# Moving the second normalisation's statistics to ScalarE and staging the front two slots earlier in a fused attention and expert kernel

## What is computed

```python
x = x + attention(layernorm(x))
#   Q, K, V = projections, 16 heads of 8; scores = Q K^T, causal mask, no softmax
#   out = (scores * causal) V, then the output projection with its bias
x = x + experts(layernorm(x))
#   probs = softmax(x @ Wg) over 8 experts, the two largest kept
#   each token's result is the sum over its two experts of
#   prob * (relu(x @ W1[e] + b1[e]) @ W2[e] + b2[e])
```

## Time and profile before

| | |
|---|---|
| runs shown | 308.76, 564.43 and 1236.85 us, median 564.43 us |
| profiled execution, span (the only time it has) | 350.7 us |
| TensorE busy | 234.8 us, 67% |
| VectorE busy | 207.1 us, 59% |
| ScalarE busy | 140.9 us, 40% |
| GpSimd busy | 198.4 us, 57% |
| TensorE's granted clock, mean | 0.854 of full speed |

### The profile page before, as it was taken

One profiled execution on the slowest core, in us unless ns is written; L12 is line 12 of the kernel. 1 busy time (PEld: TensorE's weight loads), 2 busy tenths in 40 slices (PEclk: granted clock), 3 DMA queues, 4 the chain that ended last, 5 costly groups with the idle time before them and its releaser, 6 DMA issues.

```text
span 350.7 us, 6314 instructions
## 1 busy us (share of the span) xinstructions
PE 234.8 (67%) x1320; PEld 174.7 (50%) x1320; DVE 207.1 (59%) x745; ACT 140.9 (40%) x509; POOL 198.4 (57%) x184
## 2 busy tenths in 40 slices
PE   0799999999998999574300685977677686665000
PEld 0345666666565655363100675976567685554000
DVE  6888887989898989654541043434333443343074
ACT  2434566566565554342200363444343544342000
POOL 3465644588888888744673045554564455646300
PEclk9999999999999999855555599689898989999555
DMA  7910000000010101101121332223223232201199
GB/s 218 304 57 0 3 0 3 3 31 30 31 33 30 33 30 33 53 31 38 39 84 60 72 99 70 71 71 76 68 72 84 62 78 65 81 28 39 50 358 317
DMA packets 32399, 25.48 MB, mean 73 GB/s; under 512 B 4305, under 2 KB 30169, under 8 KB 32364
## 3 DMA queue, kind: packets, MB, share of 16 engines
q1 hardware_dynamic: 23808, 14.52, 15.2%
q0 software_dynamic: 4320, 8.47, 7.6%
q10 hardware_dynamic: 4236, 2.10, 2.0%
HBM read 13.92 MB, written 11.61 MB: 73 GB/s over the span
## 4 chain that ended last, share of the span: by engine, by line
issue 52%; PE 27%; DMA 5%; SPq 4%; ACT 3%; DVE 2%; ACTq 1%; another core or an unknown queue 1%; POOL 1%; DVEq 1%; POOLq 0%
PE ps L824 14%; PE ps L832 9%; PE ps L817 4%; DMA back<-returned 3%; ACT hT L458 3%; SPq L271 2%; SPq L289 2%; DMA bias_bc<-b_o 1%; DMA returned<-y_sb,xt 1%; POOL outer L324 1%; DMA xt<-dispatched 1%; DMA dispatched<-padding 1%; PE ps L709 0%; DVEq L243 0%
## 5 line engine op out<-in xcount | busy, mean ns | idle before, releaser
L349 POOL DMA_INDIRECT returned<-y_sb,xt x71 | 70.2, 988 | 70.9 <-DVE y_sb L685 51.3
L324 POOL TENSOR_TENSOR outer<-qkv 128x1024 f32<-128x1024 f32 x32 | 62.6, 1957 | 32.4 <-ACT qkv L404 32.0
L340 POOL DMA_INDIRECT dispatched<-rows,slot x64 | 62.5, 976 | 25.1 <-issue 15.4
L680 DVE TENSOR_TENSOR yb<-ps,b_bc 128x128 f32<-128x128 f32 x71 | 20.7, 291 | 77.2 <-PE ps L832 32.8
L824 PE MATMUL ps<-xT,w_of 128*128 128x128 f32 x284 | 51.1, 308 | 18.7 <-ACT hT L458 12.5
L739 PE MATMUL ps<-outer,causal 128*128 128x512 f32 x128 | 62.4, 610 | 0.0
L832 PE MATMUL ps<-w_sb,hT 128*128 x284 | 50.0, 304 | 16.3 <-ACT hT L458 10.3
L452 ACT ACTIVATE xT<-ps 128x128 f32<-128x128 f32 x71 | 19.8, 279 | 91.7 <-PE ps L817 72.1
L824 PEld LDWEIGHTS ps<-xT,w_of 128*128 128x128 f32 x284 | 42.8, 216 | 23.0 <-ACT xT L452 16.4
L832 PEld LDWEIGHTS ps<-w_sb,hT 128*128 128x128 f32 x284 | 42.3, 214 | 20.1 <-issue 19.9
L458 ACT ACTIVATE hT<-ps,b_col 128x128 f32<-128x128 f32 x142 | 44.4, 370 | 4.7 <-remote 3.0
(11 more groups left out here) (115 smaller groups left out, 355.5 us busy)
## 6 DMA issues: line engine op xcount, KB each, us to landing
xt<-dispatched SPq DMA_DIRECT2D x71, 65.0 KB
back<-returned SPq DMA_DIRECT2D x8, 512.0 KB, 7.6
x_sb<-x SPq DMA_DIRECT2D x8, 256.0 KB, 5.2
out<-x_sb ACTq DMA_DIRECT2D x8, 256.0 KB, 6.6
returned<-y_sb,xt POOLq DMA_INDIRECT x71, 2.3
w_sb<-w SPq DMA_DIRECT2D x1, 1024.0 KB, 5.6
w_sb<-w SPq DMA_DIRECT2D x2, 512.0 KB, 7.2
dispatched<-rows,slot POOLq DMA_INDIRECT x64
```

The lines of the kernel that those rows point to most:

```text
L324: pool.tensor_tensor(outer[:, g % OUTER_RING, :].rearrange("p (h b a) -> p h b a", h=HEADS, b=DH), k, v, ALU.mult).then_inc(outer_done, 1)
L340: pool.indirect_dma_start(out=dispatched[:, :], out_offset=bass.IndirectOffsetOnAxis(ap=slot[:, g * K + k:g * K + k + 1], axis=0), in_=row ...
L349: pool.indirect_dma_start(out=returned[:, :], out_offset=bass.IndirectOffsetOnAxis(ap=xt[:, n % G, D:D + 1].bitcast(I32), axis=0), in_=y_s ...
```

## The change

The statistics of the second normalisation leave VectorE. ScalarE now makes the negated mean with an `Identity` that scales by -1/128 and accumulates over the row, and the sum of squared deviations with a `Square` whose bias is that mean and which accumulates too. The Ln takes 1/128 as its scale. The shift becomes an `Identity` on ScalarE, and so do the four instructions that write the probabilities; these have lag 13 on ScalarE. ScalarE's and TensorE's front stages have lags smaller by two, `outer` gets a ring of 4 and `qkv` one of 12, and the waits that guard shared banks are moved by the same two tiles. GpSimd's list is as before.

```diff
-    OUTER_RING = 3
-    QKV_RING = 2 * T
+    OUTER_RING = 4
+    QKV_RING = 3 * T
...
+            def mean2_out(g):
+                wait(act, x2_done, g + 1)
+                act.activation(unread[:, 0, :], tile(g), ACT.Identity, scale=-1.0 / D,
+                               accum_out=mean2[:, g:g + 1]).then_inc(mean2_done, 1)
+
+            def spread2_out(g):
+                wait(act, mean2_done, g + 1)
+                act.activation(unread[:, 1, :], tile(g), ACT.Square, bias=mean2[:, g:g + 1],
+                               accum_out=spread2[:, g:g + 1]).then_inc(spread2_done, 1)
...
+            def shift2_out(g):
+                wait(act, rstd2_done, g + 1)
+                act.activation(norm2[:, g, 1:2], mean2[:, g:g + 1], ACT.Identity, scale=norm2[:, g, 0:1]).then_inc(norm2_done, 1)
+
+            def chosen(g):
+                if g % T < T - 1:
+                    return
+                b = g // T
+                wait(act, ids_done, 1)
+                wait(act, grec_done, b + 1)
+                for u in range(T):
+                    act.activation(rows[:, g + 1 - T + u, :, D + 1], top[:, u, 0:K], ACT.Identity,
+                                   scale=grec[:, u:u + 1]).then_inc(chosen_done, 1)
...
-            tile_slots([(10, variance_log2), (12, exponentials), (10, scale2_out), (2, qkv_out), (11, xn2T_out), (1, xnT_out), (6, qT_out), (10, rows_out),
-                        (0, normalize), (7, oT_out), (0, deviations_ahead)], N)
+            tile_slots([(10, mean2_out), (12, exponentials), (10, spread2_out), (0, qkv_out), (10, variance_log2), (11, xn2T_out), (10, scale2_out),
+                        (-1, xnT_out), (10, shift2_out), (6, qT_out), (10, rows_out), (-2, normalize), (7, oT_out), (13, chosen),
+                        (-2, deviations_ahead)], N)
...
             def scales_ahead(g):
-                if g == 2:
+                if g == 0:
                     scale1_out(2)
...
                 wait(dve, exp_done, b + 1)
+                wait(dve, chosen_done, T * b)
...
-            tile_slots([(6, stats2_out), (6, mean2_out), (5, add_residual), (9, softmax_end), (1, attend_sum),
-                        (8, softmax_start), (0, attend), (0, scales_ahead), (9, places), (6, shift2_out),
-                        (2, state_out)], N)
+            tile_slots([(5, add_residual), (9, softmax_end), (1, attend_sum), (8, softmax_start), (0, attend), (0, scales_ahead),
+                        (9, places), (2, state_out)], N)
...
-            tile_slots([(3, running_sums), (11, gate), (5, q_transposed), (7, o_transposed), (5, sum_state), (1, project),
-                        (0, transpose1), (10, transpose2), (7, project_out), (12, rank)], N)
+            tile_slots([(3, running_sums), (11, gate), (5, q_transposed), (7, o_transposed), (5, sum_state), (-1, project),
+                        (-2, transpose1), (10, transpose2), (7, project_out), (12, rank)], N)
```

More of the change, by code:

```diff
@@ L116, in preln_linear_attention_moe @@
         oT = sb("oT", [P, RING, P])
-        stats2 = sb("stats2", [P, N, 6])
-        mv2 = sb("mv2", [P, N, 2])
+        mean2 = sb("mean2", [P, N])
+        spread2 = sb("spread2", [P, N])
+        unread = sb("unread", [P, 2, D])
         norm2 = sb("norm2", [P, N, 2])
@@ L193, in preln_linear_attention_moe @@
         att_mm, x2_done = sem("att_mm"), sem("x2_done")
-        stats2_raw, stats2_done, log2_done, rstd2_done, norm2_done = (
-            sem("stats2_raw"), sem("stats2_done"), sem("log2_done"), sem("rstd2_done"), sem("norm2_done"))
+        mean2_done, spread2_done, log2_done, rstd2_done, norm2_done = (
+            sem("mean2_done"), sem("spread2_done"), sem("log2_done"), sem("rstd2_done"), sem("norm2_done"))
         rows_done, T2_done, xn2T_done, lg_mm = sem("rows_done"), sem("T2_done"), sem("xn2T_done"), sem("lg_mm")
@@ L377, in deviations_ahead @@
                     deviation1(1 if g == 0 else 2)
+            def mean2_out(g):
[6 more added lines that the diff above has]
+                               accum_out=spread2[:, g:g + 1]).then_inc(spread2_done, 1)
             def variance_log2(g):
-                wait(act, stats2_done, g + 1)
-                act.activation(log2[:, g:g + 1], mv2[:, g, 1:2], ACT.Ln, bias=eps[:, 0:1]).then_inc(log2_done, 1)
+                wait(act, spread2_done, g + 1)
+                act.activation(log2[:, g:g + 1], spread2[:, g:g + 1], ACT.Ln, bias=eps[:, 0:1], scale=1.0 / D).then_inc(log2_done, 1)
             def scale2_out(g):
@@ L502, in add_residual @@
                 dve.tensor_tensor(tile(g), ps_att, tile(g), ALU.add).then_inc(x2_done, 1)
[L504 to L515, removed]
             def attend(g):
@@ L570, in softmax_end @@
                 dve.reciprocal(grec[:, :], gsum[:, :]).then_inc(grec_done, 1)
-                wait(dve, grec_done, b + 1)
-                wait(dve, ids_done, 1)
-                for u in range(T):
-                    dve.tensor_scalar(rows[:, g + 1 - T + u, :, D + 1], top[:, u, 0:K], grec[:, u:u + 1], None,
-                                      ALU.mult).then_inc(chosen_done, 1)
                 wait(dve, pick_done, b + 1)
@@ L701, in transpose1 @@
                 wait(pe, xnT_done, g)
-                wait(pe, oT_done, g - 6)
+                wait(pe, oT_done, g - 8)
                 pe.transpose(ps_T1, xn[:, g % RING, :], ident[:, :]).then_inc(T1_done, 1)
@@ L707, in project @@
                 wait(pe, qkv_done, g)
-                wait(pe, shift_done, batches(g - 10))
+                wait(pe, shift_done, batches(g - 12))
                 pe.matmul(ps_qkv, xnT[:, g % RING, :], wqkv_sb[:, :], start=True, stop=False)
@@ L716, in q_transposed @@
                 wait(pe, qkv_done, g + 1)
-                wait(pe, xnT_done, g + 5, N)
+                wait(pe, xnT_done, g + 7, N)
                 wait(pe, qT_done, states(g) - 1)
@@ L769, in gate @@
                 wait(pe, xn2T_done, g + 1)
-                wait(pe, qkv_done, g + 10, N)
+                wait(pe, qkv_done, g + 12, N)
                 wait(pe, shift_done, batches(g - 1))
```

## The result

The changed kernel takes **313.34 us** (median of 4 runs, 312.35 to 314.35). The kernel before took 308.76 and 309.13 us in its two undisturbed runs beside it, and 564.43 and 1236.85 in two others; none of its 109 later runs was above 358.4, so those two are not the kernel's own time. The ratio of the undisturbed runs is **1.013, interval 1.011 to 1.016**: slower by 4.1 us by the ratio (4.4 by the medians), small but clear of the noise. I had forecast 311 us and a ratio of 1.007.

What follows compares the result with a forecast made beforehand. GpSimd was taken to bound 68 to 139 us, then the drain to the last rank. 350.7 + 1.5 + 1.0 = 353.2 us, ratio 1.007, put on 308.76 gives 311 us; range 299 to 620 us.

Steps and rivals of the forecast that it cites:

- What bounds the kernel: Whole kernel: TensorE full up to 68 us, GpSimd sets the pace to 139 us, then the drain decides.
- From 139 us on the drain to the last rank decides: Tail: the count of rows at 174.41 us and 15.63 us of padding, not GpSimd's list, set the first load.
- a floor: GpSimd must be done before the first load; without its two stands its last dispatch would end near 179.5 us.
- First dispatch +1.5 us: Start of GpSimd's dispatches: later, waiting for ScalarE's probabilities, some 70 us against 68.35; bounds -1 and +3.
- Nothing from 68 to 139 us: Middle: no time change, since ScalarE's 3.9 us a tile stays under GpSimd's 4.42.
- The costs of the new instructions: ScalarE: mean 273 ns, square 356, shift and probabilities 285 each, accumulated output 202; sum 1.60 us a tile.
- The rival in which ScalarE becomes the bound: At 4.72 us a tile ScalarE passes GpSimd's 4.42: 17.8 us slower, ratio 1.051 or 324 us; chance 0.26.
- The drain +1.0 us: Seven slots after the last running sums: four times -0.3, +2.7 and -0.5 us; bounds -8 and +5.
- The four gains of 0.3 us: Drain: some 0.3 us saved in each of four slow slots, the exchange with VectorE being gone.
- The rival that the drain gets shorter and faster: Fewer handoffs remove waits, so the count comes up to 8.0 us sooner: ratio 0.979 or 302 us; chance 0.36.
- the likeliest case: Whole kernel: time within 2% of an undisturbed 308.76 us, chance 0.38; range for undisturbed runs 299 to 324 us.
- the start's term: Front: two more rounds before the first running sums cost 4.6 us there, +1.5 us at GpSimd's first dispatch.

Runs made afterwards that it cites:

- e0: The kernel before, no edit, profiled where it takes about 309 us: 309.74 us, ratio 1.000.
- e13: The changed kernel repeated, no edit, beside the kernel before: 313.65 us, ratio 1.013.
- e1: The changed kernel with the front's lags, rings and guards put back as before, so only the work moved to ScalarE remains: 311.58 us, ratio 1.007.
- e2: The kernel before with only the lead of two slots and the longer rings; statistics and probabilities stay on VectorE: 315.42 us, ratio 1.020.
- e3: The changed kernel with the probabilities written by VectorE again, where it wrote them before: 316.93 us, ratio 1.025.
- e14: The changed kernel with the front staged one slot sooner instead of two: 310.73 us, ratio 1.005.
- e16: The changed kernel with eight spare copies on ScalarE ahead of the last batch's exponentials: 314.99 us, +1.3 us against the changed kernel.
- e15: The changed kernel with two spare outer products on GpSimd near the end of its list: 317.94 us, +4.3 us against the changed kernel.
- e17: The changed kernel with a one-slot lead and batches 5 to 7's probabilities on VectorE behind places; 346.3 us, ratio 0.987, where the kernel before takes 351 to 354 us.
- e7: The changed kernel with the probabilities on VectorE, behind the places: ratio 1.027, where the kernel before takes 351 to 354 us.

## Why the prediction was wrong, step by step

In condition A the way to the first load fits one sum in every profile. First dispatch, last dispatch, the difference, the stands, and what is left of GpSimd's own work, all starts in us:

| | first | last | between | stands | own work | first load |
|---|---|---|---|---|---|---|
| before (e0) | 70.62 | 181.50 | 110.88 | 1.11 | 109.8 | 184.81 |
| changed | 70.60 | 184.15 | 113.55 | 3.86 | 109.7 | 187.45 |
| changed (e13) | 72.62 | 185.99 | 113.37 | 3.90 | 109.5 | 189.29 |
| no lead (e1) | 69.42 | 182.71 | 113.29 | 3.81 | 109.5 | 186.01 |
| lead alone (e2) | 71.59 | 186.68 | 115.09 | 5.65 | 109.4 | 189.98 |
| writes on VectorE (e3) | 71.31 | 187.04 | 115.73 | 6.15 | 109.6 | 190.35 |
| lead of one (e14) | 68.19 | 181.57 | 113.38 | 3.90 | 109.5 | 184.88 |

The own work is 109.4 to 109.8 us whatever the kernel, and the first load comes 3.30 or 3.31 us after the last dispatch starts in all seven. The two free terms are the first dispatch and the stands. The sum ends at the first load: from there to the end of the span it is 123.2 to 123.6 us in five of the seven, but 124.2 in e3 and 124.9 in e2 (124.4 in e16), and why those are longer stays open. Part of the first dispatch isn't the kernel's either: GpSimd's first product starts anywhere from 13.2 to 14.3 us. Counted from that product, the first dispatch stands 55.1 and 56.3 us behind it in the two profiles of the kernel before, 57.2 to 58.3 in the four that have the changed kernel's start (the two of it, e15, e16), 55.8 without the lead (e1) and 54.6 with a lead of one (e14).

**What bounds the kernel: wrong, and the step that failed.** "From 139 us on the drain to the last rank decides", with GpSimd "a floor". It rested on 15.63 us of padding. At 3.96 us the padding ends 7 us ahead of the last dispatch, and the floor is what decides. The profile of before held a warning that I passed over. SyncE's eight small writes of one kind took 15.63 us, a copy sat 2.89 us with a wait that no semaphore of the core ended, and the span was 350.7 us beside a fastest run of 308.76. I took the ratio of that profile and put it on the time of another condition. In B the order may well be as I said: the first load starts 1.0 to 2.7 us behind the end of the padding there (188.80 after 187.85 in e17, 193.58 after 191.12), and no longer 3.3 us but 3.8 to 7.4 us after the last dispatch starts. No run in B moved one of the two ends alone as e15 and e16 do in A. The change itself was not run in B.

**First dispatch +1.5 us: right in mechanism and about in size.** It waits for the probabilities at the end of ScalarE's slot 16, as foreseen: ScalarE's writes start at 69.26 us, 0.84 us long, and the dispatch stands until 70.60 (5.99 us). Counted from GpSimd's first product, as above, the changed start is later by about 2 us (57.2 to 58.3 against 55.1 and 56.3), inside my bounds of -1 and +3. The first running sums came at 20.91 us, +5.5 against 15.4 before, where I had 4.6. What I missed is that they are also slow when they come first (3.62 us in the kernel before at 16.42, 1.96 later).

**Nothing from 68 to 139 us: right**, with ScalarE at 3.59 us a tile, where I had 3.9, and VectorE at 57.07 / 16 = 3.57, where I had 3.15. I had not seen that VectorE's writes are held by GpSimd's products, so I put the gain for TensorE at nothing; it is up to 1.7 us a batch, which serves to catch up the late start.

**The costs of the new instructions: right.** Mean 300 ns (273), square 402 (356), shift 296 and writes 286 (285), the accumulated output 187 to 192 ns as an instruction of its own (202). The rival in which ScalarE becomes the bound needed 4.4 us a tile and falls by this.

**The drain +1.0 us: the term that was mis-sized, and it enters elsewhere.** The chain of a row on ScalarE takes 2.4 us in the drain (rows of the last slots at 161.09 and 163.45), as worked out (2.4), and batch 6's probabilities follow at 163.96. The rank of batch 6 then comes at 162.3 us, where it was 160.8 in the kernel before in A, and the last one at 171.1 against 168.3: +2.8, not +1.0, as the count of rows shows in the changed kernel and then in e0:

```profile
172.09 0.15 DVE L641 TENSOR_TENSOR end_row<-ps,region_of 1x8 int32<-1x8 f32 x1 [0.16 <-PE ps L811]
```

```profile
169.31 0.15 DVE L633 TENSOR_TENSOR end_row<-ps,region_of 1x8 int32<-1x8 f32 x1 [0.17 <-PE ps L803]
```

The four gains of 0.3 us didn't come: from the rank of batch 5 to that of batch 6 the kernel before took 12.0 us in A, the changed one 13.9. At the end of the drain this +2.8 costs nothing in A, since the padding ends 7 us ahead of the last dispatch. It costs on the way, because GpSimd's list waits for batches 5 and 6: stands +2.75 us. e1, which has these stands without the lead, loses 2.1 us (1.007), about half of the 4.1. The other 2.0 us go with the lead, and with its second slot: with one slot the ratio is 1.005 (e14), no worse than with none. How the stands divide between the longer chain of a row and the late probabilities wasn't tested in A; e3, with the probabilities on VectorE, still stands 2.61 us at batch 6, for ScalarE's rows.

**The rival that the drain gets shorter and faster: not seen.** The stands came from ScalarE's rows and probabilities, not from handoffs between engines: fewer handoffs, and more stands.

**The range, and luck.** 299 to 620 us held the time, and the likeliest case's own 299 to 324 would have done; the stretch to 620, for disturbed runs, wasn't needed. That 311 us came within 2.3 us of the measured time is in part luck: the start's term held roughly, but the drain's +1.0 lay on a chain that doesn't decide in A, and the stands, which carry the rest of the loss, had no term in the sum.

## What to carry to other kernels

Before the last wait of a stretch is named from one profile, see whether that profile is of the same condition as the times: here a group of transfers that lasted four times its usual time turned the order of two chains around. For an engine with one in-order list that is nowhere full by its busy share, write the time to its end as first instruction + own work + stands, and price each moved step by what it does to those two free terms. An engine that leads its partner by a fixed number of tiles gains nothing from a longer lead once another operand gates the first use. Here the second slot of lead cost 2.9 us and the first one nothing that can be measured.

## What the runs showed of the hardware

VectorE's `tensor_scalar` on SBUF data, 215 to 229 ns alone, lasted 1.0 to 1.5 us when it began during a product of GpSimd (e0, e3), and 2.54 us when it began during a dispatch with a product right behind it (e7, the four writes 2.92 us); the `tensor_reduce` and `tensor_tensor` groups beside it kept their times (1.21 us each). An accumulated output on ScalarE shows as a second instruction of 187 to 192 ns. The first running sums of the execution took 3.62 us for four products of 512 columns (3.47 in e13 and 2.35 in the changed kernel's first profile), against 1.88 to 1.98 for the later ones; the projection took 1.65 us twice ahead of them and 0.81 behind them. The clock column is 1.00 over both, so no row says why. And the same kernel took 309 or 351 to 354 us on the same two chips at different times. Of the 42.3 us between the spans of its two profiles, 33.5 lie behind the first load (157.1 us against 123.6), in the expert part; what makes the second condition stays open.
